# Identity products between the first transposes, and four moves in the order of work, in an attention and channel-mix layer

## The reference

```python
n = layernorm(x)
q, k, v = n @ Wq + bq, n @ Wk + bk, n @ Wv + bv      # 8 heads of 128
x = x + softmax(q k^T / 32) v                        # over the 4096 rows of a sequence
n = layernorm(x); p = n shifted by one row (first row: zeros)
xr, xk = mu_r * n + (1 - mu_r) * p, mu_k * n + (1 - mu_k) * p
x = x + sigmoid(xr @ W_r) * (relu(xk @ W_k)**2 @ W_v)
```

## Time and profile before

| | |
|---|---|
| median of 3 runs | 1134.53 us (1133.89 to 1134.77) |
| profiled execution | 1133.37 us |
| its span on the slowest core | 1131.8 us (core 0) |
| spans of cores 0 to 7 | 1131.8, 1131.6, 1128.4, 1131.8, 1130.4, 1130.4, 1129.6, 1130.7 |
| busy on core 0 | PE 88%, DVE 80%, ACT 74%, POOL 7% |
| chain that ended last | PE 61%, ACT 21%, issue 9%, DVE 6% |
| mean granted clock of PE | 0.993 to 0.995 of 2.4 GHz |

### The profile page before, as it was taken

The page is one execution under the profiler, slowest core; times in us unless marked ns, Lnnn a source line. Parts: engine busy times, 40 slices in busy tenths (PEclk is TensorE's granted clock), DMA queues, the critical chain, the costliest instruction groups (busy, mean ns, idle before and its releaser), DMA issues.

```text
span 1131.8 us, 20333 instructions; the slowest of 8 cores (1128.4 to 1131.8 us)
## 1 busy us (share of the span) xinstructions
PE 990.5 (88%) x7277; PEld 670.4 (59%) x7322; DVE 901.3 (80%) x932; ACT 840.3 (74%) x1113; POOL 79.8 (7%) x144
## 2 busy tenths in 40 slices
PE   4899999999998888788887888878888878999998
PEld 2444444444466666676666666666676667656654
DVE  5614755556479999999999999999999998768754
ACT  2581132223389999999999999999999998764652
POOL 2200001011000000000000000000000110110000
PEclk9899999999999999999999999999999999999999
DMA  8862324451021323213213133321330556544421
GB/s 260 259 229 66 107 81 102 130 139 46 1 50 20 60 43 58 44 21 69 43 35 60 28 60 43 53 47 24 60 52 2 122 141 196 102 120 122 121 57 76
DMA packets 65364, 94.82 MB, mean 84 GB/s; under 512 B 46172, under 2 KB 46300, under 8 KB 64096
## 3 DMA queue, kind: packets, MB, share of 16 engines
q1 hardware_dynamic: 61904, 78.80, 26.1%
q0 software_dynamic: 3360, 14.70, 8.7%
HBM read 70.40 MB, written 36.73 MB: 95 GB/s over the span
## 4 chain that ended last, share of the span: by engine, by line
PE 61%; ACT 21%; issue 9%; DVE 6%; DMA 1%; SPq 1%; ACTq 0%; DVEq 0%; POOL 0%; POOLq 0%
PE ps L369 22%; PE ps L636 14%; ACT eg L650 10%; PE ps L721 9%; PE ps L965 5%; ACT den L700 5%; PE ps L930 5%; ACT rr L704 5%; PE ps L979 5%; DVE cx L752 2%; DVE d L664 1%; DMA xs<-x 1%; ACT cx L736 1%; PE ps L606 1%; DVE eg L710 1%
## 5 line engine op out<-in xcount | busy, mean ns | idle before, releaser
L650 ACT ACTIVATE eg<-ps 128x912 bf16<-128x912 f32 x576 | 508.5, 931 | 9.2 <-PE ps L636 8.1
L721 PE MATMUL ps<-eg,vN 128*128 128x228 bf16 x2304 | 313.4, 261 | 62.2 <-DVE eg L710 57.9
L636 PE MATMUL ps<-qsl,kT 128*128 128x228 bf16 x2304 | 319.0, 260 | 46.1 <-ACT eg L650 45.5
L710 DVE TENSOR_TENSOR eg<-eg,rr 128x3648 bf16<-128x3648 bf16 x144 | 295.6, 2053 | 7.1 <-ACT rr L704 5.6
L636 PEld LDWEIGHTS ps<-qsl,kT 128*128 128x128 bf16 x2304 | 193.2, 96 | 125.9 <-issue 103.1
L721 PEld LDWEIGHTS ps<-eg,vN 128*128 128x128 bf16 x2304 | 218.8, 97 | 81.7 <-issue 76.9
L664 DVE TENSOR_TENSOR d<-eg 128x1824 bf16<-128x1824 bf16 x142 | 156.3, 1101 | 0.0
L369 PE MATMUL ps<-xnT,wk 128*128 128x512 bf16 x469 | 108.5, 388 | 2.4 <-ACT xnT L312 1.3
L325 ACT ACTIVATE kT<-ps,cvecsb 128x512 bf16<-128x512 f32 x64 | 43.7, 687 | 77.4 <-PE ps L369 68.2
L369 PE MATMUL ps<-wv,xnT 128*128 128x512 bf16 x437 | 97.2, 379 | 2.4 <-ACT wv L232 1.9
L331 ACT ACTIVATE qst<-ps,cvecsb 128x512 bf16<-128x512 f32 (+1 forms) x40 | 23.6, 602 | 95.6 <-PE ps L369 79.5
(11 more groups left out here) (81 smaller groups left out, 807.7 us busy)
## 6 DMA issues: line engine op xcount, KB each, us to landing
xt<-x SPq DMA_DIRECT2D x26, 512.0 KB, 4.1
x<-x1d SPq DMA_DIRECT2D x17, 512.0 KB, 8.0
x1d<-x SPq DMA_DIRECT2D x9, 912.0 KB, 10.2
x1d<-cx POOLq DMA_DIRECT2D x18, 456.0 KB, 7.3
out<-x SPq DMA_DIRECT2D x15, 512.0 KB, 3.0
qd<-qst SPq DMA_DIRECT2D x5, 1024.0 KB, 4.3
kst<-wk SPq DMA_DIRECT2D x16, 256.0 KB, 13.7
kst<-wq SPq DMA_DIRECT2D x8, 512.0 KB, 17.1
```

Of the source, the lines that this page charges most:

```text
L636: r = e.matmul(ps[:, (g // 2) * 512 + (g % 2) * W:(g // 2) * 512 + (g % 2) * W + W], kT[:, k * D + g * 128:k * D + g * 128 + 128], qsl[sl ...
L650: e_act[n, hf] = P.op("scalar", [tok, free], lambda e: e.activation(dst, src, AF.Exp, scale=1.0 / 32.0))
L710: u_tok[q] = P.op("vector", [r_tok[b]], lambda e: e.tensor_tensor(dst, dst, ap(rr[b % 2], h * 2 * W, [[W, 2], [0, 8], [1, W]]), op=OP.mult))
L721: r = e.matmul(ps[:, o:o + W], vN[:, k * D + g * 128:k * D + g * 128 + 128], src[:, (n % 2) * GW + g * W:(n % 2) * GW + (g + 1) * W], star ...
```

## The change

- `keep_busy(n)` puts n products of the identity matrix with itself, 512 columns each, into PSUM bank 5. Nothing reads them. They stand ahead of the transposes of tiles 0 to 7 (18, 4, 5, 3, then 1, 4, 8, 6), 5 ahead of `k_first` and 5 behind tile 7.
- The norms of tiles 5 and 7 go from DVE to ACT, with a small bias operation on DVE. The statistics of tiles 9 and 11, which use the same small buffers, wait for them.
- The loads of the value weights into the six `vst` tiles are issued behind the load of tile 10, ahead of that of tile 11, which before preceded them.
- The key maximum of chunk 5 goes from the third slot of values 5 to the first slot of keys 7, that of chunk 6 two slots further back within keys 7.
- At the start of the channel mix, the norm of its tile 1 stands on ACT ahead of the last logarithm instead of behind the reciprocal and the eviction for tile H.

```diff
@@ -272,16 +272,24 @@
 
     def ln_stats(t):
         src = xt[x_slot(t)]
-        aggr_tok[t], rstd_tok[t] = stats_ops(src, t % 4, [x_tok[t]], None)
+        aggr_tok[t], rstd_tok[t] = stats_ops(src, t % 4, [x_tok[t]], xnorm_tok[t - 4] if t in (9, 11) else None)
 
     def ln_norm(t):
         src = xt[x_slot(t)]
         sl = t % 4
-        xnorm_tok[t] = P.op(
-            "vector", [rstd_tok[t], tr_pe.get(t - 2)],
-            lambda e: e.tensor_scalar(xn[:, (t % 2) * D:(t % 2 + 1) * D], src[:],
-                                      mv[:, sl * 2:sl * 2 + 1], rstd[:, sl:sl + 1],
-                                      op0=OP.subtract, op1=OP.mult))
+        if t in (5, 7):
+            nb = P.op("vector", [rstd_tok[t]], lambda e: e.scalar_tensor_tensor(
+                nbias[:, sl:sl + 1], mv[:, sl * 2:sl * 2 + 1], -1.0, rstd[:, sl:sl + 1],
+                op0=OP.mult, op1=OP.mult))
+            xnorm_tok[t] = P.op("scalar", [nb, tr_pe.get(t - 2)], lambda e: e.activation(
+                xn[:, (t % 2) * D:(t % 2 + 1) * D], src[:], AF.Identity,
+                bias=nbias[:, sl:sl + 1], scale=rstd[:, sl:sl + 1]))
+        else:
+            xnorm_tok[t] = P.op(
+                "vector", [rstd_tok[t], tr_pe.get(t - 2)],
+                lambda e: e.tensor_scalar(xn[:, (t % 2) * D:(t % 2 + 1) * D], src[:],
+                                          mv[:, sl * 2:sl * 2 + 1], rstd[:, sl:sl + 1],
+                                          op0=OP.subtract, op1=OP.mult))
         norm_tok[t] = xnorm_tok[t]
         if 9 <= t + 3 < 32:
             load_x(t + 3)
@@ -389,6 +397,15 @@
             evict("K", 0, k, b, toks[k])
         chunk_done[0] = toks[3]
 
+    def keep_busy(n):
+
+        def pe(e):
+            r = None
+            for _ in range(n):
+                r = e.matmul(bank(5), ident[:], ap(ident, 0, [[0, 4], [1, 128]]), start=True, stop=True)
+            return r
+        P.op("tensor", [ident_tok], pe)
+
     def k_max(c):
         return P.op("vector", [kev[c]], lambda e: e.tensor_reduce(
             kmx[:, c * 8:c * 8 + 8], ap(kT, c * 4096, [[128, 8], [D, 4], [1, 128]]), axis=AX.XY,
@@ -418,6 +435,7 @@
         if t + 1 < 4:
             ln_stats(t + 1)
         ln_norm(t)
+        keep_busy((18, 4, 5, 3)[t])
         tr_tile(t)
         if t < 2:
             cast_half(2 * t, 0, "scalar")
@@ -425,15 +443,20 @@
         cast_half(j, 0, "vector")
     for j in (4, 6):
         cast_half(j, 0, "scalar")
+    keep_busy(5)
     k_first()
     ln_stats(4)
     for t in range(4, 8):
         if t + 1 < 8:
             ln_stats(t + 1)
         ln_norm(t)
+        keep_busy((1, 4, 8, 6)[t - 4])
         tr_tile(t)
+    keep_busy(5)
     for j in range(8):
         cast_half(j, 1, ("scalar", "vector")[j % 2])
+    for j in range(2, 8):
+        load_w("wv", wv_h, j, vst[j - 2], None)
 
 
     bound = {}
@@ -475,7 +498,7 @@
         no_at.setdefault(max(0, n - 2), []).append(t)
         tt_at.setdefault(n, []).append(t)
     for c in range(8):
-        at_slot = {0: 9, 6: first[("K", 7)] + 2, 7: first[("V", 6)]}.get(c)
+        at_slot = {0: 9, 5: first[("K", 7)], 6: first[("K", 7)] + 4, 7: first[("V", 6)]}.get(c)
         if at_slot is None:
             at_slot = first[("V", c)] + 2
         km_at.setdefault(at_slot, []).append(c)
@@ -492,7 +515,8 @@
         unit(kind, c, i)
         if (kind, c, i) == ("K", 0, 4):
             for j in range(8):
-                load_w("wv", wv_h, j, kst[j] if j < 2 else vst[j - 2], w_cast["wk", j, 1] if j < 2 else None)
+                if j < 2:
+                    load_w("wv", wv_h, j, kst[j], w_cast["wk", j, 1])
             for j in range(6):
                 load_w("wq", wq_h, j, kst[2 + j], w_cast["wk", 2 + j, 1])
         if (kind, c) == ("K", 2):
@@ -1008,13 +1032,13 @@
         last_sum()
         pre_tr("H")
         pre_tr(0)
+        norm_act(1)
         log_den(NB - 1)
         recip(NB - 1)
         pre_stat(2)
         scale(NB - 1, 0)
         scale(NB - 1, 1)
         first_prev()
-        norm_act(1)
         x_part(0)
         prev_part(0)
         for i in range(1, 5):
```

## The result

The change makes the kernel slightly slower. The median after is 1136.74 us over 22 runs, beside 1135.15 us over 22 runs of the kernel before on the same chip. The ratio is 1.0016 with a 95% interval of 1.0009 to 1.0022. In some executions one die shows a lower granted clock and the time is some per cent longer: medians here are over all executions, ratios over the others alone, and where the two disagree the ratio counts. Forecast were 1131.3 us and a range of 1128.0 to 1134.0, so the time lies outside the range, on the slow side. The profiled execution took 1136.91 us.

The account below looks back on a forecast made before the run. Bound by a chain of PE in the projection, ACT in the attention, PE in the channel mix. On core 1, start 1.2, key maximum 1.2 and norm 0.65 gave 3.0; 1134.53 - 3.2 = 1131.3 us, range 1128.0 to 1134.0.

Parts of the forecast that it names:

- I take 50: no cost: Value loads ahead of tile 11's: tile 11 lands at 50, below the 51.0 allowed, so zero cost.
- rivals 3 and 4: Tile 11 lands late: at 52 to 53, time 1133, chance 0.11; or at 57.8, time 1139.7, chance 0.05.
- rival 4: Tile 11 lands at 57.8; PE waits 6.7 us, then low clock some 1.7 us; 5.2 slower, 1139.7; chance 0.05.
- Start: Projection's start: keys 1 begin 1.2 us later but at full clock, tile 8's transposes at 45.7 instead of 46.94; gain 1.2.
- The clock part: Keys 1 to tile 8's transposes: 40 products at full clock take 8.6 us instead of 11.05.
- The queue on ScalarE: Evictions, two norms and transposes up to keys 1: from about 28.0, keys 1 start near 37.1, 1.2 us later.
- Key maximum: Keys 6 to tile 29's transposes: 5.62 us undisturbed; gain 4.3 on core 0, only 1.2 on core 1.
- Norm ahead of the logarithm: Passage into the channel mix: norm fits into ACT's 2.19 us idle; gain 0.65, bounds 0 and 1.07.
- The wait for the last cast: PE's wait ahead of values 0, for a cast behind keys 2's last eviction: it stays, zero gain.
- Sum: Whole kernel: core 0 gains 6.1 us, core 1 3.0; the slowest core sets the time, so 3.0 to 3.2.
- rival 5: End of attention: some core keeps the clock dip; without any 1.7 less, 1129.6; chance 0.20 shared with another rival.
- Rival 2: Ahead of keys 1: the clock falls again, the start loses 1.2 instead of gaining 1.2, time 1133.7; chance 0.14.

Follow-up runs that it names:

- the best version: The changed kernel with the value loads put back and the norms of tiles 5 and 7 back on VectorE: 1127.36 us, ratio 0.9947 to the kernel before.

## Why the prediction was wrong, point by point

**The step that failed: "I take 50: no cost", the landing of tile 11.** Its statistics start at 55.1 as a mean and at 56.7 on core 0, right behind the landing, and by the prediction anything behind 51.0 costs (as late as tile 8 came, anything behind 52.1). Two numbers in it were wrong. The six loads were counted from 39, when SP has issued them, as if nothing were in the queue. But tile 9 landed only at 42.7 on core 0 (33.08 + 9.65, the first of the two pieces of the chain), and tile 10 was still behind it. From there eight transfers of 0.524 MB, 4.19 MB, had to move until tile 11 was in. And the rate was taken as 360 GB/s from one stretch of 2 us, where the row above has 316 over the whole of it. 42.7 + 4.19 / 0.316 = 56.0, beside 56.6, the landing; in that time 4.39 MB were moved, so nearly all of it was these eight. Both the 316 and the 42.7 come from the trace after. The page that the prediction named (the Trainium skill, DMA: Bandwidth & Descriptors, Queues, rings and completion order) has each DMA engine consume a ring in order, so that tile 11's transfer stands behind all loads ahead of it, and the runs with three, five and six of them agree; what went wrong was what I put into the sum, not that rule.

The prediction had the mechanism as rivals 3 and 4, with a chance of 0.16 together. The reckoning behind rival 4 was right: norm 10 starts 1.63 us and ends 2.44 us behind the start of tile 11's statistics, forecast 2.45. The low clock behind the wait adds 1.7 us on cores 2, 3, 5 and 6, as rival 4 had it, 2.9 on core 0 and nothing on the other three. Measured, the loss is 4.2 us in the changed kernel between tile 8 and values 0, 3.0 of them the wait, and 4.5 us of the time by the loads alone.

**Start: forecast a gain of 1.2 us, measured a loss of 0.3, most of the difference not the start's own.** Keys 1 start at 38.5, forecast 37.1. Tile 4 landed 0.95 us later than before as a mean; from the landing on, the start gains 0.6 us up to tile 8. The clock part was right: 40 products in 8.6 us, forecast 8.6. The queue on ScalarE was right in kind and almost in size: from tile 4's eviction to keys 1 9.3 us on core 0 against 9.1 forecast. What was off is where it starts: I put that eviction at 28.0, and it was at 29.96. On core 0 tile 4 landed 1.7 us later than the 22.8 that I took over from the kernel before. The landing is 22.2 to 22.8 as a mean in the six kernels without identity products and 22.5 to 23.7 in the ten with them; whether the products have a part in that is open. The lower bound of 35.9 for keys 1 was not reached by any kernel with a norm on ScalarE. With both on VectorE keys 1 start at 35.5 where tile 4's transposes come at 27.1, and at 36.8 where they come at 28.3; in the latter the gain at tile 8 is 1.4 us (45.35 against 46.73).

**Attention: not in the prediction, a term put at nothing, 0.9 us lost.** The two norms shift ScalarE's stream, and three pauses of 0.25 us in its last third come with that, on all eight cores.

**Key maximum: right.** 5.62 us forecast and measured on every core. The prediction took core 1's gain of 1.2 as the one that counts; most cores lay near it, and the mean gain of the stretch is 2.0 us. The kernel with this part alone gained 2.4 us, between the forecasts for core 1 and core 0.

**Norm ahead of the logarithm: right in kind, 0.4 to 0.5 instead of 0.65**, and below what the time can tell. It passes on to `diff`, whose wait falls from 1.07 to 0.43. ScalarE's wait before the last logarithm was 2.19 on core 0, but 0.87 on cores 5 to 7, less than the norm's 1.23. Where it is so short the norm holds the logarithm up by 0.1 us (6.8 us from the last reciprocal but one to the last becomes 6.9), which the prediction missed. The wait is 1.39 us after on the cores with the long passage and none on the others, forecast about 1.

**The wait for the last cast** stays, 1.9 us, as forecast.

**Sum, as means.** Forecast for a core like core 1 was 3.0 less. Measured is 2.55 more. Of these 5.6 us, 4.2 are the loads, 1.5 the start (of which 0.95 the later landing of tile 4), 0.9 the attention and 0.2 the norm, while the key maximum and what follows it up to the first score gave 1.0 more than the 1.2 counted for core 1. That makes 5.8; the rest is of the size of one core fewer with the long passage that rival 5 speaks of.

**Rival 2** (the clock falls again before keys 1) is refuted for the products, and without products it is what happens. **Rival 5** (luck at the end of the attention) holds. The passage from the last reciprocal but one to the last takes 8.4 us on some cores, with the granted clock at 0.8 as its mean, and 6.8 to 6.9 on others, at 1.0. 5 of 8 cores had the long one before, 4 after, 0 or 1 in five of the kernels, and 2 to 7 in the other nine. It may not be luck alone: in the six kernels whose attention takes 636.2 us 28 of 48 cores have it, in the ten others 22 of 80. No run separates the two. A part of what the best version gains, 1 core instead of 5, may be of this kind.

## What to carry to other kernels

A load that is moved ahead of another one is paid for in bytes by the one behind. Count them from the landing of what is already in the queue, not from the issue, at the lowest rate that the trace shows near there, and compare with the time at which the late one is due; here three of six were free and each further one delayed the landing by about 2 us. Work that is moved to a less busy engine is not free when that engine also serves the same short chain: norm, transposes and eviction of a tile are one chain, and two of its three steps on ScalarE were dearer than on two engines. And take a change apart before judging it: of these five parts two gained, one was below the noise, two lost, and the sum was 0.16% slower where the best selection of them is 0.5% faster.

## What the runs showed of the hardware

ScalarE pauses for 0.17 to 0.27 us without waiting for anything in a few blocks of the attention, six blocks or a multiple of six apart. Which blocks these are depends on the instructions that stand ahead of them in ScalarE's stream, waits included, hundreds of us earlier. It is the same on all cores of a kernel but for one block or two, and it made the same stage 635.2 to 635.4 us long in some kernels and 636.2 in others. Pauses stand 64 activations or a multiple of it apart, and a transfer of 8192 bytes on the queue called instruction follows most of them by 0.8 to 2.2 us.

Products of an identity matrix with itself, which nobody reads, are worth 5 us to a kernel with two norms on ScalarE whose first products otherwise run at the low clock: 1.0032 without against 0.9987 with them. The stage that they are put in accounts for 4.3 us of it (values 0 at 80.34 without, 76.08 with them), of which 1.6 lie ahead of keys 1. With the norms on VectorE they are worth 2 to 3 us (0.9974 without, 0.9947 and 0.9956 with them). Which of the groups of products are needed was tested only for the one ahead of tile 6.
